# A value product that shares its PSUM bank with a sequence's small products, and three banks for the scores by key

## The chip, the cores and the metric

One core of one Trainium2 chip. The metric is the device time of one launch in microseconds, the median of the runs. TensorE, VectorE (DVE), ScalarE (ACT), GpSimd (POOL) and the queue of SyncE (SP) each work through their own list of instructions in order and wait on semaphores for one another.

## What is computed

```python
def _L0_attn_ref(x, W_qkv, W_out):          # x: 16 sequences, 512 positions, 128 features; 16 heads of 8
    qkv = jnp.einsum('bsd,ndh->bnsh', x, W_qkv)
    q, k, v = jnp.split(qkv, 3, axis=-1)
    attn = jnp.einsum('bnqh,bnkh->bnqk', q, k) * scale
    attn = jax.nn.softmax(attn + mask, axis=-1)          # causal
    out = jnp.einsum('bnqk,bnkh->bnqh', attn, v)
    out = out.reshape(B, -1, S)
    return jnp.einsum('bds,nhd->bsd', out, W_out)
...
x = x + _L0_attn_ref(_layernorm(x, axis=-1), L0_attn_W_qkv, L0_attn_W_out)
x = x + _L0_ffn_ref(_layernorm(x, axis=-1), ...)         # each token goes to 2 of 8 experts, weighted
```

The second line routes each of the 8192 tokens by a softmax over 8 logits; its experts have 512 hidden features, a GELU, a sigmoid gate, a residual and a normalisation of their own.

## The kernel before

The program has three stages: attention with the routing beside it, the experts over 71 blocks of 256 rows, and the sum of both experts' outputs. The change is in the first.

**Groups and batches.** A batch is one sequence of 512 positions; its 16 heads are worked in four groups of four. So there are 64 groups, and the loop of groups writes each engine's instructions by one table, `SLOT`. The table has four lines, for the four groups of a batch. I call the stretch of the program that one line makes a **place**: place 0 to place 3. A token stands for a step, and each engine emits its own part of the step where the token stands. `AHEAD` says for which group a step is: in the place of group s the A's are those of group s+3, the B's those of s+1, PV, OT, RC and ON those of s. `BATCH_OF` says for which batch: Q, K, xT two batches ahead, V one ahead, the routing one or two behind.

**The steps.**
- A0 to A5: scores by query into `sa` (four banks, two at a time), a mask by a small matmul, and on DVE the maximum over keys (`neg_max`), six reductions a group. A step waits until the reduction two steps back has read its banks (`sa_read`).
- mT, mE, mW, mR: the maxima are transposed on TensorE, copied out by DVE, stored to DRAM and read back as a row of `q_stack` (two transfers on SP). B0 waits for the second.
- B0 to B11: scores by key into `st`, the exponential on ACT into `probs`, the causal mask on GpSimd. A B waits until the exponential of the B two before has read its bank (`exp_done`).
- PV0 to PV3: the value product, by blocks of 128 keys, four heads side by side, all into the bank `pv`. OT transposes `pv` to `o_t` on DVE; RC takes the reciprocal of the sums; ON multiplies on GpSimd and stores. PV0 waits for the OT of the group before (`pv_read`).
- SR loads a group's q and k from DRAM, ST stores a batch's q and k there (four transfers, after Kl), AR reads a batch's attention output back, and `out` adds it to x on GpSimd.
- ln, rs1, xn: layer norm of a row, statistics on DVE, the power and the scaling on GpSimd. xT transposes `xn` on TensorE, ACT copies it to `xnT`. Q and K are matmuls of `xnT`; ACT rounds the product to `q_hi`, DVE writes the rest to `q_lo` (Ql, Kl). V is the third.
- ln2, rs2, zn, zT, LG, LGa, Ra, EX, Rb, Rc, Rd, CM, Re, Rf: second layer norm, logits, top two experts (chains of short DVE instructions), ranks by CM, and the rows' addresses. S0 to S7 scatter the rows by GpSimd's DMAs.

**The bank `misc`.** xT, Q, K, V, zT, LG and CM write it in turn. `MISC_ORDER` lists the uses in program order, and `misc_free` makes TensorE wait before each until the reader of the use before is done: ACT's copy for xT, zT and V, DVE's subtraction for Q and K (`lo_done`), the addition of the bias for LG (`logits_done`), the addition on `slot` at the start of Rf for CM (`rank_done`).

Of the kernel before, what the change touches and what calls it, by code (L numbers as in the profile page):

```python
# [5 lines left out]
def attention_and_routed_experts(nc, x, w_qkv, w_out, wr, br, wi, bi, wg, bg, wo, bo, gamma, beta, out,  # L6
# [8 lines left out]
    B, S, D = x.shape  # L15
# [3 lines left out]
    P = 128  # L19
    NT = S // P  # L20
    G = 4
# [11 lines left out]
    with ctx:  # L33
# [8 lines left out]
        def sem(name):  # L42
# [77 lines left out]
        misc = pb("misc", [P, S])  # L120
# [27 lines left out]
        b_part = sb("b_part", [P, 3, 3 * D], BF16)  # L148
        b_rest = sb("b_rest", [P, 3 * D])
        sa = pb("sa", [P, 2, 2, S])  # L150
        st = pb("st", [P, 2, S])
        pv = pb("pv", [P, S])

        x_loaded, w_loaded = sem("x_loaded"), sem("w_loaded")
        x_all_loaded = [sem(f"x_all_loaded{k}") for k in range(2)]
# [34 lines left out]


        SLOT = {
# [4 lines left out]
        }  # L197
        AHEAD = {"SR": 4, "A": 3, "mT": 2, "mE": 2, "mW": 2, "mR": 2, "B": 1, "PV": 0, "OT": 0, "RC": 0, "ON": 0}
        BATCH_OF = {"ln": 2, "rs1": 2, "xn": 2, "xT": 2, "Q": 2, "Ql": 2, "K": 2, "Kl": 2, "ST": 2, "V": 1, "XL": 0,
# [36 lines left out]
        MISC_USERS = ("xT", "Q", "K", "V", "zT", "LG", "CM", "BU")  # L236
        MISC_ORDER = [(kind, n) for kind, _, n in ORDER + TAIL if kind in MISC_USERS]

        def misc_use(kind, b):
            return MISC_ORDER.index((kind, b)) + 1  # L240

# [31 lines left out]

        def pe_sequence(pe, kind, k, n):
            if kind == "zT":
                misc_free(pe, "zT", n)
                pe.wait_ge(ln2_done, n + 1)
                transposes(lambda i: xn2[:, n % 2, i, 0:D])
            elif kind == "LG":
                misc_free(pe, "LG", n)  # L280
                pe.wait_ge(zT_done, n + 1)
                for i in range(NT):
                    last = nc.tensor.matmul(misc[:, i * E:(i + 1) * E], xn2T[:, i * P:(i + 1) * P],
                                            wr_sb[:, :], start=True, stop=True)
                last.then_inc(misc_written, 1)
            elif kind == "CM":

                if n == 0:
                    pe.wait_ge(r_const, made["upper, onesb"])
                misc_free(pe, "CM", n)  # L290
                pe.wait_ge(chosen_done, n + 1)
                nc.tensor.matmul(misc[:, 0:(NT + 1) * E], upper[:, :], chosen[:, :, :].rearrange("p t e -> p (t e)"),
                                 start=True, stop=True)
                for i in range(NT):
                    last = nc.tensor.matmul(misc[:, (i + 1) * E:(NT + 1) * E], onesb[:, :],
                                            chosen[:, i, :].unsqueeze(1).broadcast_to([P, NT - i, E]),
                                            start=False, stop=True, skip_group_check=True)
                last.then_inc(misc_written, 1)
# [83 lines left out]
                last = pool.tensor_scalar(dst(i), src(i), nm_[:, i:i + 1], rs_[:, i:i + 1], ALU.add, ALU.mult)  # L382
            last.then_inc(ready, 1)

        def misc_free(pe, kind, b):
            at = misc_use(kind, b) - 1
            if at:
                before, b_ = MISC_ORDER[at - 1]
                done, count = {"xT": (xT_done, b_ + 1), "Q": (lo_done, 2 * b_ + 1), "K": (lo_done, 2 * b_ + 2),
                               "V": (vaug_done, b_ + 1), "zT": (zT_done, b_ + 1), "LG": (logits_done, b_ + 1),  # L390
                               "CM": (rank_done, b_ + 1), "BU": (b_up_done, 1)}[before]
                pe.wait_ge(done, count)
# [214 lines left out]
        def _(pe):  # L607
# [20 lines left out]
            def b_step(n, t):  # L628

                third, j, g = t // G, HEAD_OF[t % G], n % NG  # L630
                if t == 0:
                    pe.wait_ge(max_landed[g], 16 * (n // NG + 1))
                if n > 0 or t >= 2:
                    pe.wait_ge(exp_done, NB_ * n + t - 1)
                for kk, at, w in ([(0, 0, 512)], [(1, 0, 384)], [(3, 0, 256), (2, 256, 256)])[third]:
                    last = nc.tensor.matmul(st[:, t % 2, at:at + w], k_pad[:, G * g + j, kk * P:(kk + 1) * P],  # L636
                                            q_stack[:, g, S - w:S], start=True, stop=True)
                last.then_inc(st_written, 1)

            def pv_part(n, kk):  # L640
                b, g = n // NG, n % NG
                if kk < 3:
                    pe.wait_ge(masked, NB_ * n + G * (kk + 1))
                if kk == 0:
                    pe.wait_ge(vaug_done, b + 1)
                    pe.wait_ge(pv_read, n)
                for j in range(G):
                    w = S - kk * P
                    last = nc.tensor.matmul(pv[R * j:R * j + R, kk * P:S], v_aug[:, b % 2, kk, G * g + j, :],  # L649
                                            probs[:, n % 2, j, PT_OFF[kk]:PT_OFF[kk] + w],  # L650
                                            start=(kk == 0), stop=True, skip_group_check=True)
                if kk == NT - 1:
                    last.then_inc(pv_written, 1)
# [5 lines left out]
            for kind, k, n in ORDER:  # L659
                pe_sequence(pe, kind, k, n)  # L660
                if kind == "A":
                    a_step(n, k)
                elif kind == "B":
                    b_step(n, k)
                elif kind == "PV":
                    pv_part(n, k)
                elif kind == "mT":
                    pe.wait_ge(sa_read, NA * (n + 1) + (1 if n + 1 < GROUPS_ALL else 0))
                    nc.tensor.transpose(sa[0:G * NT, 0, 1, S - P:S],
                                        neg_max[:, n % 2, :, :].bitcast(F32).rearrange("p j i -> p (j i)"),  # L670
                                        ident[:, :]).then_inc(maxT_written, 1)
                elif kind == "xT":
                    misc_free(pe, "xT", n)
                    pe.wait_ge(ln1_done, n + 1)
                    transposes(lambda i: xn[:, i, :])
                elif kind in ("Q", "K"):
                    misc_free(pe, kind, n)
                    pe.wait_ge(xT_done, n + 1)
                    nc.tensor.matmul(misc[:, :], (wq if kind == "Q" else wk)[:, :], xnT[:, :],
                                     start=True, stop=True).then_inc(misc_written, 1)  # L680
                elif kind == "V":
                    misc_free(pe, "V", n)
                    for i in range(NT):
                        last = nc.tensor.matmul(misc[:, i * P:(i + 1) * P], xnT[:, i * P:(i + 1) * P], wv[:, :],
                                                start=True, stop=True)
                    last.then_inc(misc_written, 1)

        @block.scalar
        def _(act):
            act.wait_ge(consts, 2)  # L690
            for kind, k, n in ORDER:
# [12 lines left out]
                elif kind == "V":  # L704
                    act.wait_ge(misc_written, misc_use("V", n))
                    if n >= 2:
                        act.wait_ge(pv_written, NG * (n - 1))
                    nc.scalar.activation(v_aug[:, n % 2, :, :, 0:HD],
                                         misc[:, :].rearrange("p (i n h) -> p i n h", i=NT, h=HD),
                                         ACT.Copy).then_inc(vaug_done, 1)  # L710
                elif kind == "B":
                    third, j = k // G, HEAD_OF[k % G]
                    if k == 0 and n >= 2:
                        act.wait_ge(pv_written, n - 1)
                    act.wait_ge(st_written, NB_ * n + k + 1)
                    lo, w, at = ((0, 512, 0), (512, 384, 0), (896, 384, 128))[third]
                    nc.scalar.activation(probs[:, n % 2, j, lo:lo + w], st[:, k % 2, at:at + w],  # L717
                                         ACT.Exp).then_inc(exp_done, 1)

        @block.vector  # L720
# [118 lines left out]
        @block.tensor  # L839
        def _(pe):  # L840
            for kind, k, n in TAIL:
                pe_sequence(pe, kind, k, n)
                if kind == "BU":
                    misc_free(pe, "BU", n)
                    pe.wait_ge(bias_loaded, 16 * 11)
                    nc.tensor.transpose(misc[:, 0:2 * E * FC], b_rows[:, :], ident[0:2 * E * FC, 0:2 * E * FC])\
                        .then_inc(misc_written, 1)
# [390 lines left out]
```

## Time and profile before

| | |
|---|---|
| median of 3 runs | 1310.53 us (1308.95 to 1314.0) |
| profiled execution | 1312.31 us, of which the span from first to last instruction is 1310.3 us |
| mean granted TensorE clock | 0.954 |
| TensorE matmul busy | 1104.3 us, 84% |
| DVE busy | 987.5 us, 75% |
| GpSimd busy | 787.8 us, 60% |
| ACT busy | 740.5 us, 57% |

The page says how long each engine was busy, in bands of a fortieth of the span, and which groups of instructions cost most. Its shares are means over three stages with different limits, so what the change does is read from a stretch of the attention stage: from the instructions in order of time, and from what each waited for.

### The profile page before, as it was taken

What the parts mean: (1) busy time and instruction counts of PE and PEld (TensorE: products, weight loads), DVE (VectorE), ACT (ScalarE), POOL (GpSimd) and SP (SyncE); (2) the same over time, 40 slices, a digit from 0 to 9 for tenths busy, and PEclk for the clock granted to TensorE, in tenths of its full rate; (3) what the DMA queues carried; (4) which work ended last, traced back from release to release, by engine and by line L of the source; (5) the groups of instructions that cost most, each with busy time, mean ns of one, the idle gap of its engine ahead of it and who ended that gap; (6) DMA issues with size and microseconds to landing.
All of it is one profiled execution on the core that took longest, in us unless ns stands there. A gap on an engine that the chain in (4) does not pass through costs nothing. (4 is left out here: it accounts for less than half of the span.)

```text
span 1310.3 us, 27443 instructions
## 1 busy us (share of the span) xinstructions
PE 1104.3 (84%) x8654; PEld 830.9 (63%) x8654; DVE 987.5 (75%) x2802; ACT 740.5 (57%) x1663; POOL 787.8 (60%) x1453
## 2 busy tenths in 40 slices
PE   1699988988998988998989998329999999999920
PEld 0465555655665655655655654129999999999920
DVE  4566777777777777777777775357888888888849
ACT  0155545555555545555555555238888888888810
POOL 1146665765775765775775776554666666666630
PEclk9999999999999999999999999659999999999965
DMA  2334345334334334334324331341111111111138
GB/s 64 100 111 125 130 131 151 123 103 123 115 92 137 109 83 133 112 83 137 109 83 138 115 84 34 92 123 34 51 56 52 50 53 56 50 50 56 32 98 306
DMA packets 144413, 127.37 MB, mean 97 GB/s; under 512 B 71848, under 2 KB 104624, under 8 KB 144272
## 3 DMA queue, kind: packets, MB, share of 16 engines
q1 hardware_dynamic: 133328, 103.59, 27.2%
q0 software_dynamic: 8640, 17.84, 4.1%
q10 hardware_dynamic: 2304, 4.20, 0.8%
q8 instruction: 72, 1.18, 0.4%
q14 instruction: 69, 0.57, 0.1%
HBM read 71.13 MB, written 54.43 MB: 96 GB/s over the span
## 5 line engine op out<-in xcount | busy, mean ns | idle before, releaser
L717 ACT ACTIVATE probs<-st 128x384 f32<-128x384 f32 (+1 forms) x768 | 379.3, 525 | 317.1 <-PE st L636 314.9
L759 DVE TENSOR_REDUCE neg_max<-sa 128x2 fp32r<-128x1024 f32 (+3 forms) x384 | 390.9, 1030 | 184.2 <-PE sa L623 184.0
L591 POOL TENSOR_SCALAR_AFFINE_SELECT probs<-probs 128x128 f32<-128x128 f32 (+1 forms) x768 | 243.3, 332 | 165.6 <-ACT probs L717 158.1
L636 PE MATMUL st<-q_stack,k_pad 128*128 128x256 f32 (+2 forms) x1024 | 324.6, 391 | 15.8 <-DMA q_stack<-max_scratch 8.8
L619 PE MATMUL sa<-k_pad,q_stack 128*128 128x256 f32 (+2 forms) x1024 | 244.2, 341 | 14.0 <-DVE neg_max L759 8.3
L636 PEld LDWEIGHTS st<-q_stack,k_pad 128*128 128x128 f32 x1024 | 170.5, 191 | 117.4 <-ACT probs L717 64.7
L649 PE MATMUL pv<-probs,v_aug 128*32 128x512 f32 (+3 forms) x2048 | 168.6, 448 | 33.0 <-DVE o_t L772 26.1
L997 POOL DMA_INDIRECT y_scratch<-z,to_row x142 | 170.6, 1202 | 35.9 <-issue 35.9
L619 PEld LDWEIGHTS sa<-k_pad,q_stack 128*128 128x128 f32 x1024 | 157.9, 192 | 37.1 <-DVE neg_max L759 16.3
L1031 PE MATMUL up<-xt_hi,w_cur 128*128 128x256 f32 x568 | 167.8, 295 | 0.0
L1032 PE MATMUL up<-xt_lo,w_cur 128*128 128x256 f32 x568 | 161.7, 285 | 0.0
L1033 PE MATMUL up<-xt_hi,w_cur 128*128 128x256 f32 x568 | 161.4, 284 | 0.0
L1045 PE MATMUL y_ps<-wo_sb,hid 128*128 x1136 | 150.1, 282 | 0.0
L271 POOL DMA_INDIRECT rows_scratch<-xn,dest x128 | 129.1, 1008 | 24.4 <-issue 23.2
L991 POOL TENSOR_TENSOR inv_dev<-inv_dev,minus_half 128x2 f32<-128x2 f32 x71 | 75.8, 1067 | 106.2 <-DVE inv_dev L1151 106.1
L1045 PEld LDWEIGHTS y_ps<-wo_sb,hid 128*128 128x128 f32 x1136 | 138.8, 193 | 0.8
L1115 DVE SCALAR_TENSOR_TENSOR hid<-gate,gelu 128x512 f32<-128x512 f32 x142 | 97.8, 689 | 44.9 <-ACT gate L1085 44.9
L623 PE MATMUL sa<-maskneg,identb 128*128 128x128 bf16 (+1 forms) x768 | 124.7, 245 | 0.0
L1085 ACT ACTIVATE gate<-up,b_cur 128x256 f32<-128x256 f32 x284 | 122.3, 501 | 0.0
L1082 ACT ACTIVATE gelu<-up,b_cur 128x256 f32<-128x256 f32 x284 | 120.0, 485 | 1.6 <-PE up L1033 1.5
L649 PEld LDWEIGHTS pv<-probs,v_aug 128*32 128x32 f32 x2048 | 56.0, 111 | 100.8 <-POOL probs L591 51.8
L1031 PEld LDWEIGHTS up<-xt_hi,w_cur 128*128 128x128 f32 x568 | 109.8, 193 | 1.2 <-ACT w_cur L1068 0.4
(158 smaller groups left out, 1528.6 us busy)
## 6 DMA issues: line engine op xcount, KB each, us to landing
q_stack<-q_scratch SPq DMA_DIRECT2D x64, 256.0 KB, 2.6
k_pad<-k_scratch SPq DMA_DIRECT2D x256, 64.0 KB, 2.4
xg<-rows_scratch SPq DMA_DIRECT2D x71, 130.0 KB, 2.1
q_scratch<-q_hi SPq DMA_DIRECT2D x16, 512.0 KB, 3.1
k_scratch<-k_hi SPq DMA_DIRECT2D x16, 512.0 KB, 3.0
y<-y_scratch SPq DMA_DIRECT2D x16, 512.0 KB, 5.8
q_scratch<-q_lo SPq DMA_DIRECT2D x17, 256.0 KB, 3.2
k_scratch<-k_lo SPq DMA_DIRECT2D x17, 256.0 KB, 3.8
```

The costliest lines, as they stand in the source:

```text
L271: pool.indirect_dma_start(rows_d, bass.IndirectOffsetOnAxis(dest[:, n % 2, k:k + 1], 0), xn2[:, n % 2, k % NT, :], None).then_inc(rows_sto ...
L591: pool.affine_select(out=blk, in_=blk, compare_op=ALU.is_ge, fill=0.0, base=0, pattern=[[0, w], [1, P]], channel_multiplier=-1).then_inc(m ...
L619: nc.tensor.matmul(sa[:, s % 2, h // each, at:at + width], q_stack[:, g, i * P:(i + 1) * P], k_pad[:, G * g + j, 0:width], start=True, sto ...
L636: last = nc.tensor.matmul(st[:, t % 2, at:at + w], k_pad[:, G * g + j, kk * P:(kk + 1) * P], q_stack[:, g, S - w:S], start=True, stop=True)
L649: last = nc.tensor.matmul(pv[R * j:R * j + R, kk * P:S], v_aug[:, b % 2, kk, G * g + j, :], probs[:, n % 2, j, PT_OFF[kk]:PT_OFF[kk] + w], ...
L717: nc.scalar.activation(probs[:, n % 2, j, lo:lo + w], st[:, k % 2, at:at + w], ACT.Exp).then_inc(exp_done, 1)
L759: V.tensor_reduce(neg_max[:, n % 2, heads[0]:heads[-1] + 1, i], scores[:, :, 0:(i + 1) * P], AX.X, ALU.max, negate=True).then_inc(sa_read, 1)
L997: pool.indirect_dma_start(y2_d, bass.IndirectOffsetOnAxis(to_row[:, u, h:h + 1], 0), z[:, u % NR, h, :], None).then_inc(scattered[u % NR], 16)
L1031: nc.tensor.matmul(dst, lo, xt_hi[:, b2, :], start=True, stop=False)
L1032: nc.tensor.matmul(dst, hi, xt_lo[:, b2, :], start=False, stop=False)
L1033: last = nc.tensor.matmul(dst, hi, xt_hi[:, b2, :], start=False, stop=True)
L1045: last = nc.tensor.matmul(y_ps[h][:, :], hid[:, u % 2, c, h * P:(h + 1) * P], wo_sb[:, bass.ds(e * (FC * D) + c * D, D)], start=False, sto ...
```

## The change

`pv` is no bank of its own any more: it is `misc`. The bank that this frees goes to `st`, which has three. B of step t waits for the exponential three before, not two. PV0 is a user of the shared bank: `BANK_ORDER` is the list of all its uses, each PV0 among them, and `bank_free` waits for the reader of the use before, which for a value product is its transpose (`pv_read`). `MISC_ORDER` remains for the counts of `misc_written`. The table of places is written anew: PV0 stands beside PV1 to PV3 behind B9, OT right behind them, and the small products, `out`, the scatters, ON and `xn`/`zn` are at other points. `LAST` is the same.

```diff
-        st = pb("st", [P, 2, S])
-        pv = pb("pv", [P, S])
+        st = pb("st", [P, 3, S])
+        pv = misc
...
-            1: "SR A0 B0 B1 PV0 S0 B2 A1 B3 mT mE A2 B4 mW S1 B5 A3 B6 B7 A4 ln2 B8 S2 B9 PV1 PV2 PV3 mR rs2 B10 A5 B11 OT RC zn ON",
...
-            3: "SR A0 Ra B0 B1 PV0 S6 B2 A1 B3 mT mE A2 EX xT B4 mW S7 B5 A3 Rb Q B6 B7 A4 Ql B8 B9 PV1 PV2 PV3 K mR B10 A5 Kl ST B11 OT RC ON",
...
+            1: "SR A0 B0 B1 out S0 B2 A1 B3 mT mE A2 S1 B4 mW B5 A3 S2 B6 B7 A4 ln2 S3 B8 B9 PV0 PV1 PV2 PV3 OT mR rs2 B10 A5 RC B11 ON zn",
...
+            3: "SR A0 Ra B0 B1 B2 A1 B3 mT mE A2 EX xT B4 mW B5 Q A3 Rb Ql B6 B7 K A4 Kl ST B8 B9 PV0 PV1 PV2 PV3 OT mR B10 A5 RC B11 ON",
...
+        BANK_ORDER = [(kind, n) for kind, k, n in ORDER + TAIL if kind in MISC_USERS or (kind == "PV" and k == 0)]
...
-        def misc_free(pe, kind, b):
-            at = misc_use(kind, b) - 1
+        def bank_free(pe, kind, b):
+            at = BANK_ORDER.index((kind, b))
             if at:
-                before, b_ = MISC_ORDER[at - 1]
-                done, count = {"xT": (xT_done, b_ + 1), "Q": (lo_done, 2 * b_ + 1), "K": (lo_done, 2 * b_ + 2),
+                before, b_ = BANK_ORDER[at - 1]
+                done, count = {"PV": (pv_read, b_ + 1),
+                               "xT": (xT_done, b_ + 1), "Q": (lo_done, 2 * b_ + 1), "K": (lo_done, 2 * b_ + 2),
...
-                if n > 0 or t >= 2:
-                    pe.wait_ge(exp_done, NB_ * n + t - 1)
+                if n > 0 or t >= 3:
+                    pe.wait_ge(exp_done, NB_ * n + t - 2)
...
-                    last = nc.tensor.matmul(st[:, t % 2, at:at + w], k_pad[:, G * g + j, kk * P:(kk + 1) * P],
+                    last = nc.tensor.matmul(st[:, t % 3, at:at + w], k_pad[:, G * g + j, kk * P:(kk + 1) * P],
...
-                    pe.wait_ge(pv_read, n)
+                    bank_free(pe, "PV", n)
```

TensorE before, in place 3 of a batch in the middle, from A4 on (`sa` scores by query, `st` by key, `misc` with `wk` is K; 128x384 in `st` are B4 to B7, 128x256 B8 to B11). Q stands seven rows further up:

```order
L619 MATMUL sa<-k_pad,q_stack 128x256 x4
L623 MATMUL sa<-maskneg,identb 128x2x128 x2
L636 MATMUL st<-q_stack,k_pad 128x256 x4
L649 MATMUL pv<-probs,v_aug 32x384 x4
L649 MATMUL pv<-probs,v_aug 32x256 x4
L649 MATMUL pv<-probs,v_aug 32x128 x4
L679 MATMUL misc<-xnT,wk 128x512
L636 MATMUL st<-q_stack,k_pad 128x256 x2
```

TensorE after, in place 3, from Q (`wq`) to the value product, which now goes to `misc`:

```order
L682 MATMUL misc<-xnT,wq 128x512
L622 MATMUL sa<-k_pad,q_stack 128x384 x2
L626 MATMUL sa<-maskneg,identb 128x128 x2
L639 MATMUL st<-q_stack,k_pad 128x384 x2
L682 MATMUL misc<-xnT,wk 128x512
L622 MATMUL sa<-k_pad,q_stack 128x256 x4
L626 MATMUL sa<-maskneg,identb 128x2x128 x2
L639 MATMUL st<-q_stack,k_pad 128x256 x4
L652 MATMUL misc<-probs,v_aug 32x512 x4
L652 MATMUL misc<-probs,v_aug 32x384 x4
```

K has moved up from behind PV3 to before A4, and PV0 has moved from behind B1 to behind B9, next to PV1.

GpSimd before, the whole of place 1 from the second B on (S0 to S2 are the DMA rows, the row L377 is rs2, the four L382 are zn, the rows behind them ON):

```order
L271 DMA rows_scratch<-xn2,dest 69376x130
L591 AFFINE_SELECT probs<-probs 128x128 x3
L271 DMA rows_scratch<-xn2,dest 69376x130
L591 AFFINE_SELECT probs<-probs 128x128 x3
L591 AFFINE_SELECT probs<-probs 128x256
L271 DMA rows_scratch<-xn2,dest 69376x130
L591 AFFINE_SELECT probs<-probs 128x256
L377 TENSOR_TENSOR rstd2<-rstd2,minus_half 128x4
L591 AFFINE_SELECT probs<-probs 128x256 x2
L382 TENSOR_SCALAR xn2<-x_all,nmean2,rstd2 128x128 x4
L597 TENSOR_TENSOR r_scale<-r_den,wsum 128x16
L602 TENSOR_TENSOR o_n<-o_t,r_scale 128x128
```

GpSimd after, place 1 from `out` to B9's mask, and behind it, from rs2 to zn:

```order
L261 TENSOR_TENSOR x_all<-x_all,att 128x512
L273 DMA rows_scratch<-xn2,dest 69376x130
L594 AFFINE_SELECT probs<-probs 128x128 x2
L273 DMA rows_scratch<-xn2,dest 69376x130
L594 AFFINE_SELECT probs<-probs 128x128 x2
L273 DMA rows_scratch<-xn2,dest 69376x130
L594 AFFINE_SELECT probs<-probs 128x128 x2
L273 DMA rows_scratch<-xn2,dest 69376x130
L594 AFFINE_SELECT probs<-probs 128x256 x2
```

```order
L379 TENSOR_TENSOR rstd2<-rstd2,minus_half 128x4
L594 AFFINE_SELECT probs<-probs 128x256 x2
L600 TENSOR_TENSOR r_scale<-r_den,wsum 128x16
L605 TENSOR_TENSOR o_n<-o_t,r_scale 128x128
L384 TENSOR_SCALAR xn2<-x_all,nmean2,rstd2 128x128 x4
```

`out` has come here from place 0, a fourth scatter from place 2 (which itself has four now, and place 3 none), and zn has moved behind ON. Place 2 has the same form, with rs1 and xn. On DVE, Rc stays between A1 and mE, Rd behind A3, Rb behind A3, ln and ln2 behind A3 and A4; Ql has moved from behind A4 to behind A3 and Rb, Kl from behind A5 to behind A4, OT from behind A5 to before it.

## Rows read from the trace of the kernel before

**Rows 1.** SyncE's queue in order of time: start, us, engine, line, transfer.

```profile
258.20 0.58 SPq L446 DMA_DIRECT2D q_scratch<-q_hi  x1
...
743.38 0.58 SPq L446 DMA_DIRECT2D q_scratch<-q_hi  x1
```

**Rows 2.** Waits, 100 to 750 us: total, times, longest.

```profile
PEld st L636 <- ACT probs L717: 52.4, 99, 0.8
...
PE pv L649 <- DVE o_t L772: 23.4, 23, 2.3
...
PE misc L292 <- DVE chosen L355: 9.0, 12, 0.8
```

**Rows 3.** TensorE in order of time, place 1: start, us, operation, idle before.

```profile
322.69 0.73 PE L636 MATMUL st<-q_stack,k_pad 128*128 128x512 f32 x2 [0.68 <-DMA q_stack<-max_scratch]
324.20 1.07 PE L649 MATMUL pv<-probs,v_aug 128*32 128x512 f32 x8 [0.78 <-POOL probs L591]
...
327.61 0.62 PE L619 MATMUL sa<-k_pad,q_stack 128*128 128x384 f32 x2
...
328.66 0.74 PE L619 MATMUL sa<-k_pad,q_stack 128*128 128x256 f32 x4
...
330.04 1.50 PE L649 MATMUL pv<-probs,v_aug 128*32 128x384 f32 x24
...
333.33 0.71 PE L636 MATMUL st<-q_stack,k_pad 128*128 128x512 f32 x2
```

**Rows 4.** DVE in order of time, place 0.

```profile
313.49 0.18 DVE L321 TENSOR_TENSOR tmp<-pr,pm 128x32 f32<-128x32 f32 x1
...
315.04 1.80 DVE L759 TENSOR_REDUCE neg_max<-sa 128x2 fp32r<-128x768 f32 x2
...
317.76 1.22 DVE L759 TENSOR_REDUCE neg_max<-sa 128x4 fp32r<-128x1024 f32 x1
318.89 0.15 DVE L357 TENSOR_TENSOR sm<-pm 128x4 f32<-128x4 f32 x1
```

**Rows 5.** DVE in order of time, places 3, 1 and 2.

```profile
302.59 0.17 DVE L344 TENSOR_REDUCE sm<-ex 128x4 f32<-128x32 f32 x1
...
303.85 1.23 DVE L759 TENSOR_REDUCE neg_max<-sa 128x4 fp32r<-128x1024 f32 x1 [0.37 <-PE sa L623]
304.99 0.68 DVE L753 SCALAR_TENSOR_TENSOR q_lo<-misc,q_hi 128x512 fp32r<-128x512 f32 x1
...
329.67 1.23 DVE L759 TENSOR_REDUCE neg_max<-sa 128x4 fp32r<-128x1024 f32 x1 [0.20 <-PE sa L623]
...
339.37 0.85 DVE L410 BATCH_NORM_STATS2 stats<-x_row 128x6 f32<-128x128 f32 x4
...
340.92 1.21 DVE L759 TENSOR_REDUCE neg_max<-sa 128x4 fp32r<-128x1024 f32 x1
```

**Rows 6.** TensorE in order of time, the first K in the loop.

```profile
65.76 1.13 PE L679 MATMUL misc<-xnT,wk 128*128 128x512 f32 x2 [0.95 <-DVE q_lo L753]
```

**Rows 7.** GpSimd's groups by line, 100 to 750 us: busy us, mean ns, idle before.

```profile
L591 POOL TENSOR_SCALAR_AFFINE_SELECT probs<-probs 128x128 f32<-128x128 f32 (+1 forms) x640 | 202.3, 332 | 130.4 <-ACT probs L717 124.7
...
L271 POOL DMA_INDIRECT rows_scratch<-xn,dest x96 | 96.8, 1008 | 16.2 <-issue 16.2
...
L377 POOL TENSOR_TENSOR rstd<-rstd,minus_half 128x4 f32<-128x4 f32 x26 | 27.1, 1041 | 1.4
...
L382 POOL TENSOR_SCALAR xn<-x_all,nmean,rstd 128x128 f32<-128x128 f32 x52 | 22.5, 439 | 0.0
L259 POOL TENSOR_TENSOR x_all<-x_all,att 128x512 f32<-128x512 f32 x13 | 16.6, 1281 | 38.8 <-DMA att<-att_scratch 38.8
```

**Rows 8.** TensorE after a long wait, and the window 176 to 177 (clock: third last).

```profile
175.42 1.93 PE L649 MATMUL pv<-probs,v_aug 128*32 128x512 f32 x8 [2.27 <-DVE o_t L772]
...
176.00:177.00 1.00, 1.00 (x8) 0.00 (x0) 0.64 (x1) 0.00 (x0) 0.94 (x3) 0.50 0.00 0
```

**Rows 9.** DVE in order of time, in Rf of another place 0.

```profile
172.66 1.33 DVE L367 TENSOR_TENSOR tmp<-oh,slot 128x64 f32<-128x64 f32 x1
```

More of the change, by code:

```diff
@@ L275, in pe_sequence @@
             if kind == "zT":
-                misc_free(pe, "zT", n)
+                bank_free(pe, "zT", n)
                 pe.wait_ge(ln2_done, n + 1)
@@ L279, in pe_sequence @@
             elif kind == "LG":
-                misc_free(pe, "LG", n)
+                bank_free(pe, "LG", n)
                 pe.wait_ge(zT_done, n + 1)
@@ L289, in pe_sequence @@
                     pe.wait_ge(r_const, made["upper, onesb"])
-                misc_free(pe, "CM", n)
+                bank_free(pe, "CM", n)
                 pe.wait_ge(chosen_done, n + 1)
@@ L672, in _ @@
                 elif kind == "xT":
-                    misc_free(pe, "xT", n)
+                    bank_free(pe, "xT", n)
                     pe.wait_ge(ln1_done, n + 1)
@@ L676, in _ @@
                 elif kind in ("Q", "K"):
-                    misc_free(pe, kind, n)
+                    bank_free(pe, kind, n)
                     pe.wait_ge(xT_done, n + 1)
@@ L681, in _ @@
                 elif kind == "V":
-                    misc_free(pe, "V", n)
+                    bank_free(pe, "V", n)
                     for i in range(NT):
@@ L716, in _ @@
                     lo, w, at = ((0, 512, 0), (512, 384, 0), (896, 384, 128))[third]
-                    nc.scalar.activation(probs[:, n % 2, j, lo:lo + w], st[:, k % 2, at:at + w],
+                    nc.scalar.activation(probs[:, n % 2, j, lo:lo + w], st[:, k % 3, at:at + w],
                                          ACT.Exp).then_inc(exp_done, 1)
@@ L843, in _ @@
                 if kind == "BU":
-                    misc_free(pe, "BU", n)
+                    bank_free(pe, "BU", n)
                     pe.wait_ge(bias_loaded, 16 * 11)
```

4 rows, old and new, of the table SLOT are left out of this document.

## The prediction, made before the changed kernel ran

> **What bounds the kernel now.** I read the banded table of the page first: from the second slice to about 800 us TensorE is busy nine tenths of every slice and the other engines five to seven, so the attention loop is where the edit acts and TensorE is its bound. The work after it (some 500 us) keeps its instructions, apart from the waits in `LAST`, and I count it unchanged. Then the queue's own rows give the period: the store of `q_hi` comes once per sequence, at 258.20 and, ten sequences later, at 743.38, so a sequence of four groups takes 48.5 us [rows 1]. The list of waits says what stops TensorE: the value product waited 23.4 us in all for `o_t`, the transpose that empties `pv` [rows 2]. The time line of place 1 shows it in the small: B0 and B1 start at 322.69, after 0.68 us of waiting for the row of maxima, then 0.78 us idle before PV0 at 324.20; the next group starts its B0 at 333.33 [rows 3]. A modelled end hides about 0.25 us more of each such wait: two B's show 0.73 us, and a matmul behind them can start some 0.25 us before that end. So PV0's wait is 1.0 us in this group, and with recorded waits of 1.8 us per sequence (23.4 us over 53 groups, times four) and 0.25 us in each of four groups it is 2.8 us per sequence.
>
> **What goes away, per sequence.** (a) PV0 no longer waits for the transpose of the group before, since OT now stands a whole group ahead of it: -2.8 us. (b) B0 of place 1 waited 0.68 us because the loads of SR waited for the K stores; these are issued earlier now: -0.7. (c) The value product is one block, not two. PV0 (512 columns) shows 1.07 us and PV1 to PV3 (768 columns) 1.50 [rows 3]; a line through both has 0.21 us of fixed cost, some of it the modelled end: I take 0.15, and 0.1 for the B behind a value product, which starts with its weights not loaded. One block less saves 0.25 us a group: -1.0. (d) A third bank for `st`. TensorE's weight loads waited 52.4 us for the exponentials in 53 groups [rows 2], 1.0 us a group at most; TensorE's own row shows nearly none of it as idle. Bounds 0 and 1.0 us a group; I take 0.15, by the matmul row, -0.6. Sum: -5.1 us.
>
> With this, place 1 takes 10.64 - 1.0 - 0.25 - 0.15, and 0.2 for short waits on the reductions: **9.45 us**.
>
> **What is added.** `misc` now holds one thing at a time, and TensorE waits in line for each reader. All of these readers run on DVE behind reductions that TensorE itself must first feed, so each wait is a chain.
>
> Place 3, K. It waits for `q_lo` (Ql). DVE gets there by: A3 from its start to its reduction, 0.84 us (A4 needs 1.01, 328.66 to 329.67, and has 0.17 more of matmul); the reduction 0.9 (1.80 for two); Rb 0.89 (302.59 to 303.85 less the idle 0.37); Ql 0.68; signal 0.1: 3.4 us after A3's start. TensorE has only A3, B6, B7 in that time, 327.61 to 328.66, 1.05 us [rows 3, 4, 5]. K waits 2.3 us. Before, A4, B8, B9 and PV1 to PV3 stood between as well. That such a wait is real shows in the one group without that cover: K at 65.76 waited 0.95 us for `q_lo` [rows 6].
>
> Place 3, PV0. It waits for `k_lo`: A4 start to reduction 1.01, reduction 1.14 (303.85 to 304.99), Kl 0.68, signal 0.1 is 2.9 us; TensorE has A4, B8, B9, 328.66 to 330.04, 1.4 us. **1.5 us**.
>
> Place 2, PV0 waits for `logits`: from A3's start 0.84, reduction 0.9, ln 1.55 (339.37 to 340.92), A4's reduction 1.14, LGa 0.2, signal 0.1: 4.7 us; TensorE has A3 to B9 (327.61 to 330.04, 2.4 us) and LG, 0.8: **1.5 us**.
>
> Place 0. From A1's reduction on DVE runs 1.14, Rc and the copy of maxima 1.55 (313.49 to 315.04), two reductions 1.80, Rd 0.92, then A4's 1.13 and Re and the addition on `slot` 0.8 [rows 4]. A1's reduction now starts some 1.55 us after B0, since PV0 is no longer between, and A2's is done 5.2 us after B0, where A4 could start at 4.5: 0.7 us. CM waits for Rd, 1.2 us; PV0 waits for `slot`, which is ready at 9.0, with B9 done at 7.95: 1.05. Before, CM waited 9.0 / 12 = 0.75 already [rows 2], and A4 a part of its 0.7, which I put at 0.3: **+1.9**.
>
> GpSimd, places 1 and 2. Before, it came to `zn` 1 us before TensorE wanted it. Now place 1 has the addition `out` and a fourth scatter too, and `zn` stands behind ON. In order: twelve masks, 202.3 us / 640 x 12 = 3.8; out 1.28; four scatters, (96.8 + 16.2) / 96 x 4 = 4.7; rs2 1.04; zn, four times 0.44, 1.75; ON, two multiplications of which one has 128 elements per row as each of zn's, at least 0.5 [rows 7]. That is 13.1 us, begun about 1.3 us into the place when ON of the group before is done: 14.4. zT on TensorE is due at 9.45 + 2.2 = 11.65, so it waits **2.8 us**. Place 2 carries the same load less `out` (11.8 us), from 14.4 to 26.2 at the least, and its last mask waits for B11, near the end of the place; xn then ends some 27.5. Place 2 is 15 us long by this sum and xT is due at 26.7: about 1.0 us, and Q then waits 0.35 for `xnT`. Place 2's and 3's share: 4.2 us.
>
> Sum of what is added: 2.3 + 1.5 + 1.5 + 1.9 + 4.2 = **11.4 us** a sequence. Net +6.3.
>
> **The clock.** After 2.27 us without work (until 175.42) PV0's eight matmuls took 1.93 us, where they take 1.07, and the granted clock of 176 to 177 is 0.50, the lower of the two levels (1.2 GHz) [rows 8]. It stayed there for about 3 us, which costs 1.5. The waits before zT (2.8) and K (2.3) are as long as this one: two drops per sequence, +3 us. The DVE chains behind them start from TensorE's A3 and A4, so the loss isn't hidden. The Trainium skill ("TensorE: Matmul & The Clock Gate", HAM oscillation) tells of loops in which each such wait throttles the array anew; it speaks against the change, and by it these 3 us stand in every sequence. The rows show it for single waits only.
>
> One more place where a rule is weighed: at 172.66 a DVE product of 64 elements per row took 1.33 us, as long as GpSimd's addition (1.28) that ran at its side [rows 7, 9]. That addition now meets reductions out of PSUM in place 1. If they were held up as well the price would be up to 1.3 us a sequence, 18 us in all; I take none. The Trainium skill ("SBUF — State Buffer", Who interferes with whom) says that DVE collides with GpSimd where it reads two operands from SBUF, and not in a `tensor_reduce`; by it the sum stays as it is.
>
> **Sum.** The scatters exist for 14 of the 16 sequences: 14 x (6.3 + 3) = +130. The first two have neither scatters nor Rb at K in full, and gains and losses cancel there. Against the profiled execution, 1312.3, that is 1442; the median is 1.8 lower: **1440 us**.
>
> **Rivals.**
> 1. The clock holds: for it, the wait of 0.78 us at 324.20 was followed by matmuls of the usual length [rows 3]; against it, [rows 8]. 1312.3 + 14 x 6.3 less 2 = 1399.
> 2. GpSimd doesn't bind, because its place-1 load starts earlier or spreads better than I put it. Then zT, xT and Q wait for nothing (-4.2) and one drop (-1.5) goes: 1310.5 + 14 x 3.6 = 1361.
> 3. The third bank pays: the weight loads' 52.4 us for `st`, and those ahead of PV, were true losses. Were 2.5 us a group won in place of 0.4, the sequence would gain 8.4 more, 9.3 - 8.4 = +0.9 with the drops, and without them -2.1: 1310.5 - 14 x 2.1 = 1281. It decides from 2.0 us a group on, with the clock held. Against it: from 324.20 to 333.33 no row of TensorE carries idle time [rows 3].
> 4. Gains and added waits cancel, since the chains overlap more than my sum: 1311.
>
> **Chances.** Forecast 0.50; rival 1 0.17; rival 2 0.17; rival 3 0.07; rival 4 0.05; still slower (a third drop at place 0, whose three waits total 3.0 us in 4.6) 0.04. The forecast's own range is 1410 to 1475. With rivals 1 and 2 the range is 1350 to 1475. Measurement tells 0.5%, 6.5 us: faster 0.07, same 0.05, slower 0.88.
>
> **What would show it.** In the waits: `misc<-xnT,wk` for `q_lo` some 2.3 us in every sequence; the value product for `k_lo`, `logits` and `slot`, 1.2 to 1.5 each; the transposes into `misc` for GpSimd's `xn`, 2.8 and 1.0. `pv` for `o_t` gone. The stores of `q_hi` some 58 us apart. Granted clock below 1.00 in most sequences; place 1 near 9.5 us. I am wrong if K finds `q_lo` ready, or if `zn` ends before TensorE comes to zT.

## The result, and the profile after

The changed kernel takes **1480.55 us** (median of 4 runs, 1479.62 to 1483.03) where the one before took 1309.74: a ratio of 1.1305, 95% interval 1.1275 to 1.1335. It is slower, as forecast, and by 40 us more than forecast: 5.5 us above the upper end of the range.

| | before | after |
|---|---|---|
| span of the profiled execution | 1310.3 us | 1477.7 us |
| mean granted TensorE clock | 0.954 | 0.874 |
| TensorE matmul busy | 1104.3 us, 84% | 1171.6 us, 79% |
| DVE busy | 987.5 us, 75% | 991.1 us, 67% |
| one sequence in mid-loop | 48.5 us | 61.4 us |

The instructions are the same in number and DVE's work is the same in sum, but TensorE's matmuls show 67 us more of busy time, so some of them ran slowly.

SyncE's queue, once per sequence as in [rows 1]:

```profile
341.71 0.58 SPq L449 DMA_DIRECT2D q_scratch<-q_hi  x1
403.15 0.59 SPq L449 DMA_DIRECT2D q_scratch<-q_hi  x1
```

The list of waits, 100 to 950 us (total, times, longest). It answers to [rows 2]; the wait for `o_t` is gone from it:

```profile
PE misc L399 <- POOL xn L384: 51.9, 28, 3.1
PE misc L682 <- DVE q_lo L756: 29.0, 14, 2.1
PE misc L652 <- DVE k_lo L756: 17.8, 14, 1.5
PE misc L652 <- DVE slot L366: 13.2, 13, 1.1
PE misc L294 <- DVE chosen L357: 12.7, 13, 1.0
PE sa L622 <- DVE neg_max L762: 9.3, 15, 0.7
PE misc L652 <- DVE logits L335: 7.2, 11, 0.7
PE misc L682 <- ACT xnT L700: 6.0, 14, 0.4
```

TensorE in order of time through one sequence. Place 0 begins at 351.94, place 1 at 367.89, place 2 at 377.30, place 3 at 394.32 (the three B's of a place's start):

```profile
351.94 0.94 PE L639 MATMUL st<-q_stack,k_pad 128*128 128x512 f32 x3
...
359.13 0.18 PE L294 MATMUL misc<-chosen,upper 128*128 128x40 bf16 x1 [0.98 <-DVE chosen L357]
...
361.08 4.50 PE L652 MATMUL misc<-probs,v_aug 128*32 128x512 f32 x32 [1.11 <-DVE slot L366]
...
367.89 0.94 PE L639 MATMUL st<-q_stack,k_pad 128*128 128x512 f32 x3
...
373.18 2.36 PE L652 MATMUL misc<-probs,v_aug 128*32 128x512 f32 x32
...
377.30 0.94 PE L639 MATMUL st<-q_stack,k_pad 128*128 128x512 f32 x3
...
382.79 0.63 PE L399 MATMUL misc<-ident,xn 128*128 128x128 f32 x4 [3.08 <-POOL xn L384]
...
389.80 2.74 PE L652 MATMUL misc<-probs,v_aug 128*32 128x512 f32 x32 [0.65 <-DVE logits L335]
...
394.32 0.94 PE L639 MATMUL st<-q_stack,k_pad 128*128 128x512 f32 x3
...
397.61 0.63 PE L399 MATMUL misc<-ident,xn 128*128 128x128 f32 x4 [0.88 <-POOL xn L384]
...
403.12 1.12 PE L682 MATMUL misc<-xnT,wk 128*128 128x512 f32 x2 [2.13 <-DVE q_lo L756]
...
407.43 4.16 PE L652 MATMUL misc<-probs,v_aug 128*32 128x512 f32 x32 [1.15 <-DVE k_lo L756]
```

Every wait that the change adds stands there, at the step and with the engine that the prediction named. Look then at one kind of row: the same 32 matmuls of the value product take 2.36 us in place 1, and 4.50 and 4.16 in places 0 and 3. The windows of one microsecond say why (granted clock: third last number):

```profile
359.00:360.00 1.00, 0.84 (x9) 0.67 (x9) 1.00 (x1) 0.23 (x1) 0.00 (x0) 0.95 1.13 180
360.00:361.00 1.00, 0.00 (x0) 0.00 (x0) 0.90 (x7) 0.64 (x2) 0.67 (x2) 0.50 0.99 272
...
365.00:366.00 1.00, 1.00 (x14) 0.62 (x7) 0.37 (x1) 0.00 (x0) 0.00 (x0) 0.50 0.00 0
366.00:367.00 1.00, 1.00 (x8) 0.95 (x8) 0.35 (x1) 0.49 (x1) 0.10 (x1) 0.63 0.00 0
```

The clock stands at its lower level (0.50, 1.2 GHz) for some 6.8 us, from 359.9 to 366.7, and nearly the whole value product of place 0 falls into it. The same view has 383.8 to 390.6 for place 2 and 404.3 to 411.1 for place 3: three drops in this sequence, 6.8 us each, 20.5 us in all. Over 300 to 800 us the mean is 0.84; in the kernel before it was 1.00.

### The profile page after: what moved, and what is told of

It is laid out like the page before. It is cut to its first block and busy times, and to the rows that moved or that the text cites. A ratio compares the mean times of both kernels' runs of the same rounds, so it can differ in the third digit from the quotient of the medians.

```text
span 1477.7 us, 27443 instructions
## 1 busy us (share of the span) xinstructions
PE 1171.6 (79%) x8654; PEld 892.4 (60%) x8654; DVE 991.1 (67%) x2802; ACT 729.4 (49%) x1663; POOL 791.6 (54%) x1453
## 5 line engine op out<-in xcount | busy, mean ns | idle before, releaser
L720 ACT ACTIVATE probs<-st 128x384 f32<-128x384 f32 (+1 forms) x768 | 363.0, 528 | 431.8 <-PE st L639 428.3
L762 DVE TENSOR_REDUCE neg_max<-sa 128x2 fp32r<-128x1024 f32 (+3 forms) x384 | 397.3, 1042 | 186.7 <-PE sa L626 181.3
L594 POOL TENSOR_SCALAR_AFFINE_SELECT probs<-probs 128x128 f32<-128x128 f32 (+1 forms) x768 | 246.8, 335 | 399.3 <-ACT probs L720 388.0
L639 PE MATMUL st<-q_stack,k_pad 128*128 128x256 f32 (+2 forms) x1024 | 300.5, 389 | 6.1 <-DMA q_stack<-max_scratch 5.8
L622 PE MATMUL sa<-k_pad,q_stack 128*128 128x256 f32 (+2 forms) x1024 | 269.1, 368 | 19.0 <-DVE neg_max L762 12.9
L652 PE MATMUL misc<-probs,v_aug 128*32 128x512 f32 (+3 forms) x2048 | 203.5, 550 | 40.9 <-DVE k_lo L756 17.8
L622 PEld LDWEIGHTS sa<-k_pad,q_stack 128*128 128x128 f32 x1024 | 170.4, 207 | 59.8 <-DVE neg_max L762 27.5
L652 PEld LDWEIGHTS misc<-probs,v_aug 128*32 128x32 f32 x2048 | 77.0, 132 | 162.0 <-issue 101.9
L775 DVE STREAM_TRANSPOSE o_t<-misc 128x512 f32<-128x512 f32 x64 | 45.8, 715 | 162.4 <-PE misc L652 162.4
L626 PE MATMUL sa<-maskneg,identb 128*128 128x128 bf16 (+1 forms) x768 | 132.6, 257 | 0.0
```

The costliest lines, as they stand in the source:

```text
L594: pool.affine_select(out=blk, in_=blk, compare_op=ALU.is_ge, fill=0.0, base=0, pattern=[[0, w], [1, P]], channel_multiplier=-1).then_inc(m ...
L622: nc.tensor.matmul(sa[:, s % 2, h // each, at:at + width], q_stack[:, g, i * P:(i + 1) * P], k_pad[:, G * g + j, 0:width], start=True, sto ...
L626: last = nc.tensor.matmul(diagonal, identb[:, :], maskneg[:, :].unsqueeze(1).broadcast_to([P, each, P]), start=False, stop=True, skip_grou ...
L639: last = nc.tensor.matmul(st[:, t % 3, at:at + w], k_pad[:, G * g + j, kk * P:(kk + 1) * P], q_stack[:, g, S - w:S], start=True, stop=True)
L762: V.tensor_reduce(neg_max[:, n % 2, heads[0]:heads[-1] + 1, i], scores[:, :, 0:(i + 1) * P], AX.X, ALU.max, negate=True).then_inc(sa_read, 1)
```

## The experiments

Each comparison below is a median against the kernel before, run on the same chip with it. The runs e9 to e12 were made on another chip than the rest; the kernel before took 1311.81 us there and 1310.88 or 1311.37 on the first, so their times can be set beside the others'. No kernel leaves any of the work out; two have useless matmuls besides.

**The table alone, on the banks of before** (`e1_table_alone`). The kernel before, with all four lines of the changed table and none of its other edits; two of the lines:

```diff
-            1: "SR A0 B0 B1 PV0 S0 B2 A1 B3 mT mE A2 B4 mW S1 B5 A3 B6 B7 A4 ln2 B8 S2 B9 PV1 PV2 PV3 mR rs2 B10 A5 B11 OT RC zn ON",
...
-            3: "SR A0 Ra B0 B1 PV0 S6 B2 A1 B3 mT mE A2 EX xT B4 mW S7 B5 A3 Rb Q B6 B7 A4 Ql B8 B9 PV1 PV2 PV3 K mR B10 A5 Kl ST B11 OT RC ON",
...
+            1: "SR A0 B0 B1 out S0 B2 A1 B3 mT mE A2 S1 B4 mW B5 A3 S2 B6 B7 A4 ln2 S3 B8 B9 PV0 PV1 PV2 PV3 OT mR rs2 B10 A5 RC B11 ON zn",
...
+            3: "SR A0 Ra B0 B1 B2 A1 B3 mT mE A2 EX xT B4 mW B5 Q A3 Rb Ql B6 B7 K A4 Kl ST B8 B9 PV0 PV1 PV2 PV3 OT mR B10 A5 RC B11 ON",
```

> The new table of places on the banks of before (the value product has its own bank, st has two, misc its old order). Theory (readers' waits, GpSimd's order, clock drops): the value product's waits for k_lo, logits and slot go (1.1, 0.7, 1.1 us per sequence in the changed kernel), and the drop of the clock in place 0 with them; K's wait for q_lo (2.1), zT's for GpSimd (3.1), xT's (0.9) stay, as do the drops behind zT and K. Per sequence 61.4 - 2.9 - about 2.5 = 56 us against 48.5 before: 1395 to 1425 us. Rival, it is the sharing of the bank that costs: within 2% of before, 1310 to 1335. Rival, it is the missing third score bank: no slower than the changed kernel by more than the table explains, so above 1480.

1397.98 us, ratio 1.0682 (1.0637 to 1.0727). This is within the range given for the theory. So about half of the 170 us comes with the order alone. Of the rest, the next run tells two parts apart: sharing the bank with two score banks adds 48 us, the third score bank another 34. The waits of PV0 for the small products are gone; K's for `q_lo` stays, at most 2.1 us. Those for GpSimd are shorter (at most 1.7 us, where the changed kernel has 3.1), since B2 waits for its bank before them (24.6 us in 48 times, 100 to 750 us).

**Two score banks in the changed kernel** (`e2_two_score_banks`).

```diff
-        st = pb("st", [P, 3, S])
+        st = pb("st", [P, 2, S])
...
-                if n > 0 or t >= 3:
-                    pe.wait_ge(exp_done, NB_ * n + t - 2)
+                if n > 0 or t >= 2:
+                    pe.wait_ge(exp_done, NB_ * n + t - 1)
```

> The changed kernel with two banks for st instead of three; one bank stays empty. Theory: the third bank is worth 0.1 to 0.3 us a group where TensorE is not waiting for something else, so 0 to 20 us slower than the changed kernel: 1480 to 1500. Rival, the third bank is worth 1 us a group or more: above 1540.

1446.14 us, ratio 1.1035 (1.0991 to 1.1079): **34 us faster than with three banks**, the reverse of both expectations. Its TensorE, in order of time through places 2 and 3:

```profile
372.62 0.50 PE L639 MATMUL st<-q_stack,k_pad 128*128 128x512 f32 x1 [0.51 <-ACT probs L720]
...
376.08 0.63 PE L399 MATMUL misc<-ident,xn 128*128 128x128 f32 x4 [1.49 <-POOL xn L384]
...
381.46 2.36 PE L652 MATMUL misc<-probs,v_aug 128*32 128x512 f32 x32 [1.20 <-POOL probs L594]
...
394.36 1.12 PE L682 MATMUL misc<-xnT,wk 128*128 128x512 f32 x2 [2.13 <-DVE q_lo L756]
...
398.19 2.36 PE L652 MATMUL misc<-probs,v_aug 128*32 128x512 f32 x32 [1.53 <-DVE k_lo L756]
```

A B2 without a third bank waits 0.51 us for an exponential, in every place of this sequence. TensorE comes to zT later for it, and waits there 1.49 us, not 3.08. K waits exactly as long as before, and PV0 longer; yet both value products take 2.36 us. In this sequence only place 0 drops the clock. (The list puts PV0 of place 2 down to GpSimd; that wait ends as DVE's `logits` comes, and the masks that PV0 needs were made in the place before.) So the third bank saved waits of half a microsecond and gathered them into one long one. Over 300 to 800 us the clock is 0.94 here, against 0.84 with three banks.

Whether one wait costs the clock can't be read from its length, nor from the waits ahead of it. K's 2.13 us dropped it in the sequence of the changed kernel shown above, with 0.88 and 0.43 us idle ahead. Three sequences later in the same trace, with 0.87 and 0.42 ahead, it didn't (first fence). In this run it didn't at 394.36, with 0.43 ahead; one sequence later, with the same waits, it did, for 3.4 us (second fence):

```profile
589.11 1.13 PE L682 MATMUL misc<-xnT,wk 128*128 128x512 f32 x2 [2.13 <-DVE q_lo L756]
590.00:591.00 1.00, 1.00 (x9) 0.87 (x8) 0.02 (x1) 0.60 (x1) 0.00 (x0) 1.00 0.62 236
```

```profile
452.29 2.08 PE L682 MATMUL misc<-xnT,wk 128*128 128x512 f32 x2 [2.14 <-DVE q_lo L756]
453.00:454.00 1.00, 1.00 (x3) 0.34 (x1) 0.00 (x0) 0.00 (x0) 0.00 (x0) 0.50 0.44 168
```

What else decides it stays open.

**GpSimd's load as before** (`e3_pool_order`). The steps S0 to S7, `out`, zn and xn go back to where they stood; place 1 of it, place 2 likewise:

```diff
-            1: "SR A0 B0 B1 out S0 B2 ... mW B5 A3 S2 B6 B7 A4 ln2 S3 B8 B9 ... RC B11 ON zn",
+            1: "SR A0 B0 B1 S0 B2 ... mW S1 B5 A3 B6 B7 A4 ln2 B8 S2 B9 ... RC B11 zn ON",
```

> The changed kernel with GpSimd's load placed as before: out in place 0, scatters three in place 1, three in place 2, two in place 3, zn and xn ahead of ON. Banks and all of TensorE's order as in the changed kernel. Theory: zT's wait (3.1 us) falls below 0.5, xT's (0.9) goes, the drop behind zT goes; 3.5 us of waits and 3 us of clock in 14 sequences: 1480 - 90 = 1390 (1375 to 1410). Rival, GpSimd's order does not matter since TensorE then waits for the next reader: above 1450.

1385.37 us, ratio 1.0571 (1.0530 to 1.0612): 95 us less than the changed kernel. The transposes into `misc` are gone from its list of waits but for one of 0.9 us. This is the largest single part, and within the range of the theory. It depends on the banks, though: with two score banks the same order gives only 27 us (1446.14 to 1419.19, `e9_pool_order_two_banks` below).

**Rb behind Kl** (`e4_rest_of_q_first`).

```diff
-            3: "... B5 Q A3 Rb Ql B6 B7 K A4 Kl ST B8 ..."
+            3: "... B5 Q A3 Ql B6 B7 K A4 Kl Rb ST B8 ..."
```

> The changed kernel with Rb moved in place 3 from ahead of Ql to behind Kl. Theory: K's wait falls from 2.1 by Rb's 0.9 to 1.2 us. If the clock still drops behind it: 14 x 0.9 = 13 us, 1467; if the drop goes as well: 1420 to 1430. Rival, the wait for q_lo is made by ACT's q_hi or by A3's reduction alone: no change, 1480.

1437.26 us, ratio 1.0967 (1.0913 to 1.1021). The longest wait of K is 1.2 us, as worked out, and 43 us are gained where the waits alone give 13. The rest goes with the clock, which is 0.88 over 300 to 800 us, and of whose three drops the one behind K is gone: from 347 to 413 us it falls only in places 0, 2 and again 0, for 6.8 us each. The range for that case, 1420 to 1430, is missed by 7 us.

**The waits filled** (`e5_filled_waits`): the clock by itself, in the changed kernel.

```diff
+        FILL = {"zT": 13, "xT": 4, "CM": 4, "K": 9, "Q": 1}
+        FILL_PV = (4, 0, 2, 5)
...
+            if count:
+                pe.wait_ge(exp_done, NB_ * m + t - 2)
+            for _ in range(count):
+                nc.tensor.matmul(st[:, t % 3, :], identb[:, :], maskneg[:, :].unsqueeze(1).broadcast_to([P, NT, P]),
+                                 start=True, stop=True)
```

> The changed kernel with useless bf16 matmuls of 512 columns put ahead of the steps that wait: 13 ahead of zT, 9 ahead of K, 4 each ahead of xT and CM, 5, 2 and 4 ahead of PV0 in places 3, 2 and 0. They write the score bank that the next B overwrites, and wait only for what that B waits for. Nothing of the work is left out. Theory: the waits end when they did (the readers are on other engines), but TensorE has no long idle time, so the clock stays at 1.00 and a sequence takes 61.4 - 6.6 = 55 us in spite of 40 more matmuls: 1390 (1370 to 1410). Rival, the clock loss is small since it falls into later waits: 1460 or above.

**1400.1 us**, ratio 1.0679 (1.0649 to 1.0710), 80 us less than the changed kernel, with 42 matmuls a sequence more. The window from 300 to 800 us of it, and then of the changed kernel:

```profile
300.00:800.00 500.00, 473.35 (x3529) 300.32 (x3530) 345.88 (x776) 235.18 (x498) 303.60 (x694) 1.00 0.33 99
```

```profile
300.00:800.00 500.00, 410.99 (x2809) 270.67 (x2805) 305.96 (x683) 210.24 (x443) 268.28 (x611) 0.84 0.29 87
```

And two steps of it, ahead of which stand their useless matmuls:

```profile
363.10 2.97 PE L287 MATMUL st<-maskneg,identb 128*128 128x512 bf16 x13
366.30 0.63 PE L414 MATMUL misc<-ident,xn 128*128 128x128 f32 x4 [0.23 <-POOL xn L399]
...
382.29 2.12 PE L287 MATMUL st<-maskneg,identb 128*128 128x512 bf16 x9
384.58 1.12 PE L700 MATMUL misc<-xnT,wk 128*128 128x512 f32 x2 [0.18 <-DVE q_lo L774]
```

The readers come when they came, since they are on other engines; only the clock differs, 1.00 for 0.84. zT starts 5.45 us into place 2 where it started 5.49 us into it, and K 8.77 us into place 3 where it was 8.80. The rows of SyncE's queue put a sequence at 54.4 us. So the waits without the clock cost 5.9 us, and 61.4 - 54.4 = **7.0 us is the clock**.

**Both orders mended** (`e6_both_orders`): the table of `e3_pool_order` with Rb where `e4_rest_of_q_first` has it.

```diff
+            3: "SR A0 Ra B0 B1 S6 B2 A1 B3 mT mE A2 EX xT B4 mW S7 B5 Q A3 Ql B6 B7 K A4 Kl Rb ST B8 B9 PV0 ..."
```

> The changed kernel with both orders mended: GpSimd's load as before, and Rb behind Kl. Theory: the two are different waits and add up: 1385 less 12 to 40 (0.9 us of wait per sequence, and the drop behind K in part of them): 1345 to 1373. It stays slower than before by the waits of PV0 for k_lo, logits and slot, and of K. Rival, each mends the same critical path: 1385.

1362.67 us, ratio 1.0393 (1.0363 to 1.0423). That is in the range of the theory: apart the two gave 95 and 43 us, together they give 118. The list of waits has PV0 for `k_lo` 19.9 us, for `slot` 11.8, K for `q_lo` 16.2.

**The same table on the banks of before** (`e10_mended_table_own_bank`): what sharing costs once the orders are mended, less what the third score bank gives, which this run lacks. The kernel before, with the four lines of the table of the run above; the last of them:

```diff
-            3: "SR A0 Ra B0 B1 PV0 S6 B2 A1 B3 mT mE A2 EX xT B4 mW S7 B5 A3 Rb Q B6 B7 A4 Ql B8 B9 PV1 PV2 PV3 K mR B10 A5 Kl ST B11 OT RC ON",
+            3: "SR A0 Ra B0 B1 S6 B2 A1 B3 mT mE A2 EX xT B4 mW S7 B5 Q A3 Ql B6 B7 K A4 Kl Rb ST B8 B9 PV0 PV1 PV2 PV3 OT mR B10 A5 RC B11 ON",
```

> The table with both orders mended (1363 us with the shared bank), on the banks of before: the value product in its own, two for st. Theory: PV0 waits for no small product (1.5 for k_lo, 1.1 for slot, 0.7 for logits per sequence), and the drops of the clock in place 0 and 3 thin out: 1363 - 14 x 3.3 - some 20 of clock + up to 20 for B2's wait = 1300 to 1330. Rival, the waits only move to the next reader: above 1345.

1343.94 us, ratio 1.0229 (1.0187 to 1.0272): 19 us less, not the 33 to 63 expected. PV0's waits are gone; B2 now waits for its bank (26.0 us in 51 times), and B0 for the row of maxima (20.9 us, at most 2.7). So the truth lies at the edge of the rival's range: with the sharing gone, other waits take up much of what it gives. The table as such still costs 32 us against the one of before.

**Two score banks under GpSimd's old order** (`e9_pool_order_two_banks`) and **under filled waits** (`e12_filled_two_banks`): is a third bank slow in itself? The same edit as in `e2_two_score_banks`, with its waits, in those two kernels:

```diff
-        st = pb("st", [P, 3, S])
+        st = pb("st", [P, 2, S])
```

> The run with GpSimd's load as before (1385 us), with two score banks instead of three. On the changed kernel two banks were 34 us faster than three. Theory: that was the clock, since with three banks TensorE reached zT and K sooner and its idle time there became one long piece; with GpSimd's wait gone a second bank less can only cost B2's wait of 0.5 us a group, up to 28 us, less what the waits behind it absorb: 1385 to 1410. Rival, a third bank is slow in itself: faster than 1385 by 20 to 40 us.

> The changed kernel with the waits filled with useless matmuls (1400 us), and two score banks. Theory: with the clock held at 1.00 the third bank shows its own worth, which was hidden: not faster than 1400, 1400 to 1425. Rival, a third bank is slow in itself: 1365 to 1385.

1419.19 us where three banks gave 1385.37, and 1451.02 where three gave 1400.1. The third bank is worth 34 us in the one and 51 in the other. It isn't slow in itself, so the rivals are out, but both times lie above the ranges given (1385 to 1410, 1400 to 1425). In the second a part of the 51 is the filling: the useless matmuls waited 23.5 us for exponentials there, and end later than the wait that they fill. So the same bank is worth +34 us or -34 us, by what stands behind it.

**OT ahead of A5, in the kernel before** (`e7_before_ot_early`). Place 3 of its table; OT moves likewise in the other three:

```diff
-            3: "... K mR B10 A5 Kl ST B11 OT RC ON"
+            3: "... K mR OT B10 A5 Kl ST B11 RC ON"
```

> The kernel before with its own banks and one change: OT stands ahead of A5 in every place, so the next PV0 finds the bank read. Theory: the wait for o_t (2.8 us per sequence by the prediction) goes: 1310 - 16 x 2.8 = 1265 (1262 to 1290). Rival, DVE now holds A5's reduction back until the value product is done and A1 waits for it: 1300 to 1315.

**1288.21 us**, ratio 0.9821 (0.9789 to 0.9853). The wait for `o_t` has left the list. I had given it 45 us, and 23 came. B0's wait for the row of maxima has grown in its place, by 9 us over 100 to 750 us; first this run, then the kernel before:

```profile
PE st L636 <- DMA q_stack<-max_scratch: 18.0, 18, 2.2
```

```profile
PE st L636 <- DMA q_stack<-max_scratch: 8.8, 12, 1.7
```

Where the rest went isn't shown.

**One value block, in that kernel** (`e8_before_one_block`).

```diff
-            1: "SR A0 B0 B1 PV0 S0 B2 ... B9 PV1 PV2 PV3 mR rs2 OT B10 ..."
+            1: "SR A0 B0 B1 S0 B2 ... B9 PV0 PV1 PV2 PV3 mR rs2 OT B10 ..."
```

> The kernel before with its own banks, OT ahead of A5, and PV0 moved next to PV1 to PV3. Against the run with OT ahead alone it measures the one block: 0.25 us a group by the prediction, 16 us: 1250. Rival, the exponentials wait for TensorE through the longer block and with two score banks B2 waits 0.5 us for its bank, as it did with two banks on the changed order: 0.5 us a group worse, 1280 to 1300.

1304.38 us, ratio 0.9951 (0.9930 to 0.9971), 16 us slower than with two blocks. The rival holds, and costs a little more than its range: `st` waited 30.9 us for exponentials in 67 times, 0.5 us each. In the kernel before it was 3.0 us in 13. With two score banks PV0 between B1 and B2 is the cover for the first exponentials; that is what its place was good for.

**RC and ON early as well** (`e11_ot_rc_on_early`), the version that the runs pointed to.

```diff
-            1: "... mR rs2 B10 A5 B11 OT RC zn ON"
+            1: "... mR rs2 OT RC B10 A5 B11 ON zn"
```

> The kernel before with OT ahead of A5 (1288 us), and now RC right behind OT and ON ahead of zn and xn. In the run with OT alone TensorE waited 18.0 us for the row of maxima, 2.2 us at the worst, since SyncE's queue waits for ON before it sends that row. Theory: ON comes 0.7 us (RC ahead of A5) and in places 1 and 2 another 1.7 us sooner, so this wait goes, and zT finds xn just in time: 1265 to 1278. Rival, zn behind ON now makes zT wait (0.9 us of slack before, ON takes 0.8): 1285 to 1300.

**1284.12 us**, ratio 0.9780 (0.9745 to 0.9815). It falls between the theory's range and the rival's. The wait for the row of maxima is down to 10.3 us, not gone; zT waited 0.2 us once, so the rival's mechanism is out. Against the run with OT alone its interval overlaps, so only the gain over the kernel before, 2.2%, is certain.

## Why the prediction was right in direction and short in size

- **The added waits: right in kind, and within 0.3 us but for two of the value product's.** K for `q_lo` 2.3 foretold, 2.1 measured (29.0 / 14). zT 2.8 and 3.08. xT 1.0 and 0.88. Q for `xnT` 0.35 and 0.43. CM 1.2 and 1.0. PV0 for `slot` 1.05 and 1.0 to 1.1. PV0 for `k_lo` 1.5; here 1.15, since A4, B8 and B9 ran at the low clock and filled the wait (1.53 in the run with two banks, where they didn't). PV0 for `logits` 1.5 and 0.65, likewise: 1.4 in the run with GpSimd's old order. Place 1: 9.45 foretold, 9.41 measured.
- **The sum without the clock: right.** 48.5 + 6.3 = 54.8 us; with the waits filled 54.4. Rival 1, the clock holds, gave 1399; the run that makes it hold gives 1400.1. That it agrees to 1 us is partly luck: 14 x 5.9 is 83 us, and the run took 89 more than the kernel before.
- **The clock: the step that failed.** "It stayed there for about 3 us, which costs 1.5 ... two drops per sequence, +3 us." It stays 6.8 us, and there are three drops in most sequences: 20.5 us at the lower clock in place of 6, and +7.0 us a sequence in place of +3. I had read the length from [rows 8], where it was 3.4 us. That the waits are the cause is shown by the filled run. Why each drop lasted twice as long stays open. In places 0 and 3 a further wait (1.11 and 1.15 us) ends within the first 3.2 us of the low stretch, and in place 0 of the run with two score banks a drop lasted 6.8 us where that wait fell into it (353.1) and 3.4 where the wait was already over (472.6). But in place 2 of the changed kernel TensorE works for 5.3 us of the low stretch before its next wait (0.65 us), and that drop lasts 6.8 as well. The third drop, in place 0, I had named and given 0.04. Four more microseconds in 14 sequences are 56 us, of which 40 are the miss. The early sequences gave less: the three periods of the `q_hi` stores from the second on grew by 2.3, 4.5 and 4.1 us, not by 12.9.
- **The gains, in part mis-sized.** (a) PV0's wait for the transpose went, as foretold, and it was a gain to be had without sharing anything: 23 us in the kernel before, where the sum had 45. (b) B0's wait fell from 8.8 us in 12 times to 2.4 in 3, over a longer window. (c) The single block takes 2.36 us in place 1, where the two before show 1.07 and 1.50: 0.2 less, as counted. But with two score banks it takes away the cover of B2 and costs 16 us. (d) The third bank was taken at 0.6 us a sequence; with GpSimd's old order it is worth 34 us (2.4 us in each of 14 sequences), and in the changed kernel it costs 34, by the clock.
- **Rival 2** had the right price for GpSimd's waits and too little clock: taking them away gave 95 us, 6.8 a sequence, where it counted 5.7. Its condition, that GpSimd doesn't bind, did not hold.
- **Rival 3**, that the bank pays, is out. It needed 2.0 us a group; where the bank gains most without the filling it is 2.4 us a sequence, 0.6 a group. **Rival 4**, that gains and waits cancel, is out with a sequence of 54.4 us even at the full clock.
- The row of DVE's product beside GpSimd's addition [rows 9] has its answer. Its mean was 668 ns in 12 before; and after:

```profile
L261 POOL TENSOR_TENSOR x_all<-x_all,att 128x512 f32<-128x512 f32 x14 | 17.9, 1281 | 0.0
...
L369 DVE TENSOR_TENSOR tmp<-oh,slot 128x64 f32<-128x64 f32 x13 | 3.0, 230 | 0.5
```

The addition is as long as before and now runs beside reductions, and the product, now apart from it, takes 230 ns. The reduction that stands beside the addition in place 1, with its shapes kept apart (same view; times of one in ns), after and then before:

```profile
L762 DVE TENSOR_REDUCE neg_max<-sa 128x2 fp32r<-128x1024 f32 x114 | 139.4, 1224 | 6.6 <-PE sa L626 2.2
```

```profile
L759 DVE TENSOR_REDUCE neg_max<-sa 128x2 fp32r<-128x1024 f32 x116 | 138.6, 1194 | 54.6 <-PE sa L623 54.6
```

One takes 30 ns more than before, and even that is 3 us in all, not 1.3 us a sequence. Two of them in a row take 2.56 us in places 0, 1 and 2 alike (from 352.16, 368.12 and 377.53), and only in place 1 does the addition run beside them (369.89 to 371.17). So nothing was to be paid. The Trainium skill ("SBUF — State Buffer", Who interferes with whom) lets DVE collide with GpSimd where it reads two operands from SBUF and not in a `tensor_reduce`; the trace agrees.

What is still open, besides the length of the drops, is why the mended table on the old banks is 32 us slower than the table of before; its list names B2, the maxima and K, but they weren't taken apart.

## What to carry to other kernels

A buffer that is shared in turn between two kinds of work makes the second wait for the first one's reader, so write down for each use who reads it and how much of the waiting engine's own work lies between; here that gave most waits to within 0.3 us before any run. Count idle stretches of TensorE twice, once as time and once as clock: the eight lines of the list of waits above are some 10 us a sequence, and the low clock behind them cost 7.0 more. A buffer that lets TensorE run ahead can gather short waits into one long one. Before a resource is traded to take a wait away, try to move the reader up in its own queue: one token of order gave 23 us.

## What the runs showed of the hardware that was not expected

- The low clock lasted 6.8 us in most drops of the changed kernel from 230 to 800 us (three lasted 10.2 us, two 3.4), against 3.4 us behind the single wait of 2.27 us in the kernel before. 7.0 of 61.4 us per sequence were lost to it.
- Some 42 useless matmuls a sequence made the kernel 80 us faster, since they kept the clock at 1.00. The Trainium skill ("TensorE: Matmul & The Clock Gate", HAM oscillation) tells of a loop that is throttled anew in every turn, behind waits of some 3 to 5 us for a DMA. The trace agrees in that the drops come back in every sequence; the waits here were shorter, 3.1 us at the most.
- The same wait of 2.13 us, with the same waits ahead of it, dropped the clock in one sequence and left it at 1.00 in another of the same run.
